# Block 1's normalisation one expert sooner on VectorE, and the gates' transpose behind the second product on TensorE

## The reference, cut to what matters

```python
x = x + layernorm(memory(layernorm(x)))            # memory: retrieved, below "r"
z = layernorm(layernorm(x)) * ln_g + ln_b          # 128 features per token
logits = z @ rW + rb                               # 8 experts
probs = softmax(logits); keep the best 2; w = kept / sum(kept)
hid = gelu(z @ W1[e] + b1[e])                      # 128 -> 256, every expert
outs = hid @ W2[e] + b2[e]                         # 256 -> 128
mixed = sum over e of outs[e] * w[e]
x = x + layernorm(layernorm(x) + mixed)
```

## Time and profile before

| what | value |
|---|---|
| median of 3 runs | 185.67 us |
| the profiled execution: its own time | 185.56 us |
| its span, from the first to the last instruction | 183.7 us |
| mean granted TensorE clock | 0.990 |
| TensorE (matmul) busy | 169.1 us, 92% |
| VectorE busy | 136.9 us, 74% |
| ScalarE busy | 96.6 us, 53% |
| GpSimd busy | 25.6 us, 14% |
| memory read and written | 3.76 MB and 1.05 MB |

### The profile page before, as it was taken

One profiled execution on the slowest core, in us unless ns is written; L12 is line 12 of the kernel. 1 busy time (PEld: TensorE's weight loads), 2 busy tenths in 40 slices (PEclk: granted clock), 3 DMA queues, 4 the chain that ended last, 5 costly groups with the idle time before them and its releaser, 6 DMA issues.

```text
span 183.7 us, 3108 instructions
## 1 busy us (share of the span) xinstructions
PE 169.1 (92%) x1029; PEld 135.9 (74%) x1029; DVE 136.9 (74%) x542; ACT 96.6 (53%) x170; POOL 25.6 (14%) x37
## 2 busy tenths in 40 slices
PE   6879999998999799996999999999999999999970
PEld 6434466656745267995999999998999998999960
DVE  3899998996857827498356979856979866438693
ACT  3258776674574596252725434725435725525511
POOL 2460000000041700024000024100025100002011
PEclk9999999999999999999999999999999999999996
DMA  5992000000000000000000000100000100000100
GB/s 116 306 334 59 5 0 4 0 0 2 0 0 4 2 0 0 4 0 0 0 4 0 2 0 4 57 0 0 5 0 0 57 5 0 0 4 2 57 29 29
DMA packets 3567, 4.99 MB, mean 27 GB/s; under 512 B 352, under 2 KB 2016, under 8 KB 3552
## 3 DMA queue, kind: packets, MB, share of 16 engines
q1 hardware_dynamic: 3552, 4.81, 8.4%
HBM read 3.76 MB, written 1.05 MB: 26 GB/s over the span
## 4 chain that ended last, share of the span: by engine, by line
PE 71%; DVE 18%; issue 4%; ACT 3%; POOL 1%; DMA 1%; DVEq 0%; ACTq 0%; POOLq 0%
PE bank L380 65%; DVE stats L873 4%; PE bank L388 4%; DVE mv L876 2%; DVE xn_tok L886 2%; POOL rstd L333 1%; DMA x_tok<-in_x_dram 1%; DVE xn_tok L1042 1%; PE bank L546 1%; DVE xnT L1137 1%; DVE vpe L881 1%; PE bank L537 1%; DVE h_tok L886 1%; ACT sig L809 1%; ACT L790 1%
## 5 line engine op out<-in xcount | busy, mean ns | idle before, releaser
L1137 DVE SCALAR_TENSOR_TENSOR xnT<-bank,w_tok,xnT 128x128 f32<-128x128 f32 x112 | 31.5, 345 | 21.4 <-PE bank L380 20.8
L333 POOL TENSOR_TENSOR rstd<-vpe,minus_half 128x4 f32<-128x4 f32 (+1 forms) x25 | 22.1, 891 | 114.9 <-DVE vpe L881 103.8
L380 PE MATMUL bank<-z_hi,fW_hi 128*128 128x512 f32 x64 | 27.8, 434 | 0.3 <-ACT alrT L683 0.3
L380 PE MATMUL bank<-z_lo,fW_hi 128*128 128x512 f32 x64 | 25.0, 393 | 0.0
L380 PE MATMUL bank<-z_hi,fW_lo 128*128 128x512 f32 x64 | 25.0, 390 | 0.0
L380 PEld LDWEIGHTS bank<-fW_sb,sig 128*128 128x128 f32 x192 | 23.1, 192 | 0.7
L380 PE MATMUL bank<-fW_sb,sig 128*128 128x128 f32 x192 | 23.4, 275 | 0.0
L809 ACT ACTIVATE sig<-bank,early_sb 128x512 f32<-128x512 f32 x24 | 16.0, 685 | 9.8 <-PE bank L380 9.8
L380 PEld LDWEIGHTS bank<-fW_sb,k_tok 128*128 128x128 f32 x160 | 19.5, 191 | 0.8
L380 PEld LDWEIGHTS bank<-fW_sb,h1T 128*128 128x128 f32 x160 | 19.4, 191 | 0.8
L380 PE MATMUL bank<-fW_sb,k_tok 128*128 128x128 f32 x160 | 19.6, 275 | 0.0
(11 more groups left out here) (134 smaller groups left out, 271.0 us busy)
## 6 DMA issues: line engine op xcount, KB each, us to landing
fW_raw<-in_fW_dram SPq DMA_DIRECT2D x1, 1024.0 KB, 8.7
x_tok<-in_x_dram SPq DMA_DIRECT2D x3, 256.0 KB, 4.8
out_dram<-xn_tok SPq DMA_DIRECT2D x3, 256.0 KB, 2.5
early_sb<-in_early_dram SPq DMA_DIRECT2D x1, 268.0 KB, 3.7
late_sb<-in_late_dram SPq DMA_DIRECT2D x1, 264.0 KB, 5.3
x_tok<-in_x_dram SPq DMA_DIRECT2D x2, 128.0 KB, 2.6
b_raw<-in_late_dram SPq DMA_DIRECT2D x16, 4.0 KB
out_dram<-xn_tok SPq DMA_DIRECT2D x2, 128.0 KB, 1.9
```

What stands on the lines that cost most here:

```text
L333: pool.tensor_tensor(rstd[:, ln, where], vpe[:, ln, where], minus_half[:, 0:where.stop - where.start], ALU.pow).then_inc(rstd_ready[ln], 1)
L380: return pe.matmul(out_, lhsT, rhs, start=start, stop=stop)
L1137: last = dve.scalar_tensor_tensor(out=y_tok[:, t, :], in0=bank[Y_BANK[m % len(Y_BANK)]][:, i * P:(i + 1) * P], scalar=w_tok[:, t, e:e + 1] ...
```

## The change

Two things move, both around slots 0 to 2 alone; no instruction is added or removed.

```diff
@@ TensorE
                 if slot == 0:
-                    w_transpose(0)
                     pe.wait_ge(fw2_in, 16)
                     pe.wait_ge(rs2_ready, len(RETRIEVED))
...
                     for k in range(LAST, 2 * LAST):
                         output_pair(k)
+                if slot == 0:
+                    w_transpose(0)
                 if due(R_TR, slot):
                     r_transpose(due(R_TR, slot) + 1)
@@ VectorE
             for slot in range(-AHEAD, STEPS):
+                if slot == 0:
+                    run(norm_r(2))
                 if slot >= 0:
                     if slot % E == 0:
                         start_sum(slot // E)
                     if slot < WHOLE:
                         add_expert(slot)
+                if slot == 0:
+                    run(residual(2))
+                if slot == 1:
+                    norm_z(2)
...
-                if due(NORM_R, slot):
+                if slot >= E and due(NORM_R, slot):
                     run(norm_r(due(NORM_R, slot) + 1))
-                if due(RESIDUAL, slot):
+                if slot >= E and due(RESIDUAL, slot):
                     run(residual(due(RESIDUAL, slot) + 1))
-                if due(NORM_Z, slot):
+                if slot >= E and due(NORM_Z, slot):
                     norm_z(due(NORM_Z, slot) + 1)
```

## The result

The change gives **183.24 us** (median of 4 runs, 183.06 to 183.28) where the kernel before gives 185.70 (4 runs, 185.47 to 185.79): a ratio of 0.9867, with a 95% interval of 0.985 to 0.9884. The forecast was 183.2, in a range of 182.8 to 184.1. On another occasion it was 183.48 (6 runs) against 185.98 (17 runs), ratio 0.9877 (0.9845 to 0.9908).

The account below looks back on a forecast made before the run. TensorE was taken to bound the kernel. Gains of 0.56 and 2.04 less a new wait of 0.1 made 2.5 us, from 185.56 to 183.1, forecast as a median of 183.2 us, range 182.8 to 184.1.

Parts of the forecast that it names:

- What bounds the kernel: TensorE, nearly alone from 86.39 us on; reaching slot 4 sooner should bring the end forward by the same amount.
- Rival 3: An unseen TensorE wait behind slot 3 gives the gain back: 185.2 to 185.7 us, chance 0.02.
- The first wait: TensorE's wait at the gates' transpose goes with output(0) ahead of it; r_transpose(2) starts 0.56 us sooner.
- The second wait: TensorE's wait before z_transpose(2), block 1's z, goes because VectorE has z ready sooner: 2.04 us gained.
- The new wait at output(3): TensorE's output(3) waits for VectorE's add_expert(1), now behind residual(2): 0.1 us lost, between 0 and 0.3.
- Sum: First wait plus second wait less new wait: 0.56 + 2.04 - 0.1 = 2.5 us gained.
- VectorE's chain: VectorE's start times followed from norm_r(2) through start_sum, residual(2) and add_expert(1) to norm_z(2), which ends at 82.49.
- The spare time of z: z reaches TensorE at 82.55, before TensorE comes for its transpose at 83.13: 0.58 us to spare.
- Rival 1: VectorE becomes the bound in slots 0 to 3 and output(3) waits: 183.4 to 184.0, worst 184.7 us; chance 0.11.
- Rival 2: VectorE's start_sum is blocked by GpSimd's root of r and starts 0.97 us later: 184.1 us, chance 0.03.
- Rival 4: TensorE's granted clock falls to 1.2 GHz; 10 us of it would give 188.2 us; chance 0.02.

Follow-up runs that it names:

- the run without any wait there: The changed kernel with block 0's product of gates and b2 moved between slot 1's two hidden products: 183.40 us.
- the statistics alone: The changed kernel with residual(2) and norm_z(2) back at their old places, keeping the moved statistics and gates' transpose: 183.85 us.

## Why the prediction was right

**What bounds the kernel**: right. What TensorE gained at slot 4 (86.14 - 66.09 = 20.05 before, 83.88 - 66.19 = 17.69 after, so 2.36) is what the interval shrank by, to the hundredth. Rival 3 is out.

**The first wait, 0.56**: it measured 0.50. output(0) starts 0.64 sooner by the interval's clock (5.73 to 5.09 after the first hidden product) and r_transpose(2) 0.54 sooner (7.52 to 6.98). It then takes 0.40 until the next product instead of 0.36, because it still waits some hundredths for the retrieved sum (done at 73.10, and the step of 0.06 behind it): a stall that the forecast had, at a price it had left out. The 1.70 for output(0) was too short as well (71.28 to 73.06 is 1.78), which the wait for the retrieved sum hid but for 0.02.

**The second wait, 2.04**: this was taken a little large. It rests on 1.70 us for output(3), which is right ahead of a hidden product (75.67 to 77.37) and not ahead of a transpose, where the trace has 1.78 (81.83 to 83.61 in the run without any wait there; 71.82 to 73.61 in the earlier trace rows had shown it). That is 0.08 too much; 0.05 comes back because z's transpose takes 0.41 until the next product where it had waited (85.73 to 86.14) and 0.36 where it had not. With 1.78 and 0.36 behind it, slot 4 could have started at 84.13 before, so the wait was worth 86.14 - 84.13 = 2.01.

**The new wait at output(3), 0.1, with bounds 0 and 0.3**: it measured 0.14. output(3) starts 0.29 after the last hidden product instead of 0.23 (81.37 to 81.66), and needs 1.86 instead of 1.78. Its mechanism is shown from two sides: 0.30 us more on VectorE makes it 0.30 later, and 0.20 less removes it. That the product with b2 and start_sum came 0.50 sooner and not 0.56 is not its cause, since TensorE came to output(3) later than forecast by as much: it was due at 81.60, 81.50 by the interval's clock, where the forecast had 81.43. The step that was mis-sized is the one from the end of add_expert(1) to the start of output(3). The forecast put it at 0.06, read in front of z's transpose; here it is 0.15 (80.39 + 1.12 = 81.51 to 81.66), and 0.14 with two spare instructions ahead (81.82 to 81.96) and in the run of VectorE's edits alone (81.96 to 82.10). With 0.15 in the forecast's own sum, output(3) would start at 81.52 and be 0.09 late. Why this step is longer than that in front of z's transpose was not tried. The 0.1 itself was taken between two bounds without a row for it, and that it came so near is partly luck.

**Sum**: 0.50 + 2.01 - 0.14 = 2.37 against the interval's 2.36 and the forecast's 2.50. The median moved by 2.46, and on the second occasion by 2.50; that lies nearer to the forecast than the interval does, which is chance and no merit of the sum: the two profiled executions are 2.28 apart (185.56 and 183.28).

**VectorE's chain**: by the interval's clock, start_sum at 75.37 (forecast 75.31), residual(2) at 77.67 (77.61), add_expert(1) at 80.29 (80.24), norm_z at 81.44 (81.38). The spare time of z was forecast as 0.58, and the runs show 0.78 (the rows 83.52 - 82.72 = 0.80), because TensorE itself comes 0.3 later than in the forecast (83.42 against 83.13) and z only 0.07 later (82.62 against 82.55).

**Rival 1** (VectorE becomes the bound) holds in its mechanism for 0.14 us, which the forecast had as a term. **Rival 2** (start_sum blocked by GpSimd): start_sum takes 1.12 beside a root of 1.01, and the root is no longer than before: it is out for this form. The Trainium skill, page "SBUF — State Buffer", section "SBUF: two separate sides", names a two-port mode or two inputs in SBUF as the condition; start_sum reads one tensor from SBUF and one from a bank, and the trace agrees. For the form with a constant operand the runs agree in one place and not in another. Where the spare instructions began just ahead of the second root, GpSimd's two roots were 0.23, 0.63 and 1.31 us longer beside 0.27, 0.67 and 1.35 us of it. Where two of them ran at the start of the first root, neither engine was blocked for the whole of the other's instruction: the roots were 0.04 longer and the two instructions took 0.30 us instead of 0.27. By these rows no exclusive lock held there, and where the page and the rows differ the rows decide; what sets the two places apart is open. **Rival 4** (a lower clock) is out: the granted clock is 1.00 from 84 to 174 us with TensorE busy for all of it.

## What to carry to other kernels

A wait of an in-order engine, here VectorE's 2.88 us for the product with b2, is the place to put work whose result another engine (GpSimd's root) must still turn around: 1.5 us of statistics there cost nothing and took the root off the path. Price such a move by following the chain of start times, engine by engine, until the next thing that the bounding engine waits for, and look there for the second-latest input; here it was a sum moved behind the earlier work, and it came out level with TensorE's need, 0.14 us short. Take a group's pitch from a place where the same kind of instruction follows it (1.70 and 1.78 us for the same sixteen matmuls), and the step from one engine to the other from a row of the same wait: 0.06 in front of z's transpose and 0.15 in front of output(3) decided whether the sum came in time.

## What the runs showed of the hardware

- A 128x128 float32 tensor_scalar of VectorE, SBUF to SBUF, takes 0.135 us each in a row with one operation and a constant (ten in 1.35 us), and 0.26 with two operations and two columns as operands (five in 1.28, from 81.35 until norm_z at 82.63). The kernel's normalisations are all of the second kind. Whether the columns or the second operation make the difference was not tried.
- A root of GpSimd (tensor_tensor with pow, 128x4) that starts 0.04 us after the first of a row of such instructions of the first kind is longer by nearly all of their time: 1.24, 1.63 and 2.31 us beside two, five and ten of them, against 1.01 in the change. VectorE's were not slowed, 217 to 221 ns in the run with five. But two of them that ran from 80.40 on, beside a root that started at 80.50, left that root at 1.01 us, and the second of them took 243 ns. So not every overlap costs the root its time, and why is open.
- The interval between two products of TensorE repeats to 0.02 us over runs in which nothing changed on its path (107.42, 107.42, 107.40, 107.42), while the execution's time scatters by some tenths, in part with the landing of the first inputs (VectorE's first statistics start at 3.12 in one profile and at 3.88 in another). In two of the profiles, those of the statistics alone and of two spare instructions before norm_z, the granted clock of the first 20 us was lower as well (0.89 to 0.94, against 1.00). For differences under 0.3 us it is the better measure.
